# Query and key rows copied straight from SBUF rows into the SBUF stacks, in transfers of 64 KB, in a two-layer attention and expert kernel

## What is computed

```
x = x + attention0(layernorm(x), ctx, ctx)     # 16 heads of 16 channels, softmax(q.k/4 - 0.1*|t-t'|), then Wo
x = x + experts0(layernorm(x))                 # top 8 of 1024 small experts over 4 heads, plus a dense silu layer
x = x + attention1(layernorm(x), ctx, ctx)     # 16 heads, relu on q, k and v, softmax(q.k/4), no output projection
x = x + experts1(layernorm(x))                 # 8 experts of width 512, the 2 best per token
```

## Time and profile before

| | us |
|---|---|
| median of 3 runs | 1217.73 (1215.11 to 1217.9) |
| the profiled execution | 1213.62, of which the span is 1211.8 |
| PE busy in the span | 1055.4 (87%) |
| DVE busy | 788.4 (65%) |
| ACT busy | 638.7 (53%) |
| POOL busy | 474.4 (39%) |

### The profile page before, as it was taken

The page is one execution under the profiler, slowest core; times in us unless marked ns, Lnnn a source line. Parts: engine busy times, 40 slices in busy tenths (PEclk is TensorE's granted clock), DMA queues, the critical chain, the costliest instruction groups (busy, mean ns, idle before and its releaser), DMA issues.

```text
span 1211.8 us, 16920 instructions
## 1 busy us (share of the span) xinstructions
PE 1055.4 (87%) x5478; PEld 658.8 (54%) x5478; DVE 788.4 (65%) x1986; ACT 638.7 (53%) x848; POOL 474.4 (39%) x494
## 2 busy tenths in 40 slices
PE   9499899989776999999999778999999888799991
PEld 5134343434355787787777554433334334588881
DVE  3667677786489777877787334777777955244443
ACT  2146565566528667667677422565545661355550
POOL 1347777686413243343443321212323334222220
PEclk9579999999879999999999986999998998899996
DMA  7946778666999300000002330455453328222226
GB/s 186 249 148 192 228 198 264 174 206 224 255 238 233 78 1 1 1 1 1 1 1 64 103 78 1 148 165 146 117 167 93 102 63 325 66 74 71 72 62 209
DMA packets 75595, 151.71 MB, mean 125 GB/s; under 512 B 8234, under 2 KB 45356, under 8 KB 73974
## 3 DMA queue, kind: packets, MB, share of 16 engines
q1 hardware_dynamic: 62518, 99.46, 31.9%
q0 software_dynamic: 10544, 47.23, 11.2%
q10 hardware_dynamic: 2448, 3.94, 1.2%
HBM read 73.88 MB, written 76.25 MB: 124 GB/s over the span
## 4 chain that ended last, share of the span: by engine, by line
PE 55%; DVE 24%; ACT 8%; issue 6%; POOL 3%; DMA 3%; SPq 1%; ACTq 0%; DVEq 0%; POOLq 0%
PE ps L1296 14%; DVE negmax L1589 9%; PE ps L1194 7%; PE ps L1161 6%; PE ps L1140 4%; PE ps L1175 4%; PE ps L1149 4%; PE ps L1398 3%; PE ps L1375 3%; PE ps L1361 2%; PE ps L1203 1%; PE ps L1516 1%; DVE moe_w L1885 1%; DVE hl L1594 1%; DVE on L1609 1%
## 5 line engine op out<-in xcount | busy, mean ns | idle before, releaser
L1589 DVE TENSOR_REDUCE negmax<-ps 128x1 f32<-128x512 f32 x512 | 320.9, 682 | 68.9 <-PE ps L1161 67.2
L905 ACT ACTIVATE pt<-ps 128x1024 f32<-128x1024 f32 x256 | 256.4, 1026 | 129.9 <-PE ps L1175 129.1
L1161 PE MATMUL ps<-sk,sq 56*128 56x512 f32 x512 | 166.5, 460 | 48.0 <-DVE negmax L1589 24.7
L1194 PE MATMUL ps<-pt,v_aug 128*32 128x512 f32 x1024 | 142.6, 620 | 1.2 <-POOL pt L670 0.8
L1161 PEld LDWEIGHTS ps<-sk,sq 56*128 56x128 f32 x512 | 75.7, 200 | 105.3 <-DVE negmax L1589 76.3
L1175 PE MATMUL ps<-sq,sk 57*128 57x512 f32 x512 | 127.1, 489 | 2.5 <-DVE negmax L1589 1.4
L670 POOL TENSOR_TENSOR pt<-pt,near 128x256 f32<-128x256 f32 x128 | 92.3, 728 | 76.0 <-ACT pt L905 75.7
L1175 PEld LDWEIGHTS ps<-sq,sk 57*128 57x128 f32 x512 | 50.1, 190 | 101.2 <-issue 72.4
L835 POOL DMA_INDIRECT expert_out<-yo,dest x39 | 38.2, 980 | 116.2 <-ACT yo L1080 104.5
L751 POOL TENSOR_TENSOR w_first<-w_first,moe_w 128x1024 f32<-128x1024 f32 x16 | 38.1, 2379 | 105.7 <-DVE pt L1877 105.0
L1361 PE MATMUL ps<-sel,hl 128*128 128x512 f32 x256 | 71.7, 412 | 5.6 <-DVE pt L1877 5.6
(11 more groups left out here) (284 smaller groups left out, 2008.2 us busy)
## 6 DMA issues: line engine op xcount, KB each, us to landing
expert_rows<-zero SPq DMA_DIRECT2D x3, 5586.0 KB, 58.0
expert_weights_split<-wst POOLq DMA_DIRECT2D x8, 2048.0 KB, 9.4
qk_rows<-hl SPq DMA_DIRECT2D x30, 512.0 KB
sq<-qk_rows SPq DMA_DIRECT2D x60, 192.0 KB, 4.6
sk<-qk_rows SPq DMA_DIRECT2D x60, 192.0 KB, 5.1
moe_w<-in_w POOLq DMA_DIRECT2D x16, 512.0 KB, 7.1
wexp<-expert_weights_split POOLq DMA_DIRECT2D x16, 512.0 KB, 4.6
wexp<-expert_weights_split SPq DMA_DIRECT2D x4, 2048.0 KB, 17.1
```

What stands on the lines that cost most here:

```text
L905: act.activation(pt[:, 4 * (U % 2) + 2 * half:4 * (U % 2) + 2 * half + 2, :], ps[:, 2 + 2 * half:4 + 2 * half, :], ACT.Exp, scale=(BIAS, S ...
L1161: pe.matmul(ps[:, jbank(job), :], sq[r, pair, t * P:(t + 1) * P], sk[r, pair, :], start=True, stop=True).then_inc(s_job, 1)
L1194: ins = pe.matmul(ps[32 * j:32 * j + 32, OBANK, :], v_aug[:, b % 2, c, HG * g + j, :], pt[:, 4 * (U % 2) + j, :], start=(c == 0), stop=(c ...
L1589: dve.tensor_reduce(negmax[:, n % 2, col:col + 1], src, AX, ALU.max, negate=True).then_inc(s_jd, 1)
```

## The change

The DRAM tensor is gone, and so are `write_rows` and the wait for it. `stack` now copies 32 partitions of one part of `hl` (two head pairs by 16 channels) into 16 partitions by two pairs of a stack: 64 KB each, three for each of the four tiles, so 12 for a group of heads and 48 for a batch. For this the columns of the projection weights are permuted on the host so that a group's channels lie side by side. Each transfer adds 16 to `s_ld[g]`, so the counts waited for go from 64 to 192 for each batch, and ACT waits for the last group's `s_ld` before it overwrites `hl`; POOL waits for the last group of the last batch at step 41 of layer 1, where it had waited for the rows' write. The tables are new too: one `PREPARE` for all batches, `STACKS` at steps -10, -8, -4 and 0, `FINISH` one step later. At the start SP issues the 24 transfers of keys (behind three transfers of `x` and one of the context) and ACT the 24 of queries.

```
-PREPARE = {-22: ("xt", 0), -21: ("xt", 1), -20: ("k", 0), -17: ("k", 1), -16: ("q", 0), -15: ("q", 1), -13: ("v", 0), -12: ("v", 1)}
-PREPARE_SECOND = {-17: ("xt", 0), -16: ("xt", 1), -15: ("k", 0), -14: ("k", 1), -13: ("q", 0), -12: ("q", 1), -11: ("v", 0), -10: ("v", 1)}
-FINISH = {21: ("on", 0), 22: ("on", 1), 23: ("wo", 0), 24: ("wo", 1)}
+PREPARE = {-17: ("xt", 0), -16: ("xt", 1), -14: ("k", 0), -13: ("k", 1), -12: ("q", 0), -11: ("q", 1), -10: ("v", 0), -9: ("v", 1)}
+STACKS = {-10: 0, -8: 1, -4: 2, 0: 3}
+FINISH = {22: ("on", 0), 23: ("on", 1), 24: ("wo", 0), 25: ("wo", 1)}
...
-STACKS = (None, 10, 12, 12)
...
-            def write_rows(L, b, kind, s):
...
+            def stack(g, s, dst):
+                for i, part in enumerate((0, 1, 0) if dst is sq else (0, 0, 1)):
+                    at_row = HALF * s + DH * i
+                    sp.dma_start(dst[at_row:at_row + DH, 2 * g:2 * g + 2, :].bitcast(F32),
+                                 hl[2 * DH * g:2 * DH * (g + 1), s if dst is sq else 2 + s, part].bitcast(F32)).then_inc(s_ld[g], 16)
...
             def first_rows():
...
                 for s in range(2):
                     const_rows(1, s, sq)
-                sp.wait_ge(s_dw, 128 * (B + 1))
-                for g in range(NG):
-                    for s in range(2):
-                        stack(1, 0, g, s, sq)
+                for s in range(2):
+                    sp.wait_ge(s_pre, 3 + s)
+                    for g in range(NG):
+                        stack(g, s, sq)
...
-                        pool.wait_ge(s_dw, 128 * 2 * B)
+                        pool.wait_ge(s_ld[NG - 1], 192 * 2 * B)
...
-                        act.wait_ge(s_dw, 128 * (B * L + job.b))
+                        act.wait_ge(s_ld[NG - 1], 192 * (B * L + job.b))
...
             def first_stacks(g):
-                if g == 0:
-                    act.wait_ge(s_dw, 128)
-                for i, dst in ((1, sq), (3, sk)):
-                    src = rows[0, 0, i].rearrange("l (i e) t -> (l i) e t", e=NPAIR)
-                    act.dma_start(dst[HALF:HALF + BROW, 2 * g:2 * g + 2, :].bitcast(F32), src[:, 2 * g:2 * g + 2, :]).then_inc(s_ld[g], 16)
+                for s in range(2):
+                    if g == 0:
+                        act.wait_ge(s_jd, at[0, "q", 0, s].done)
+                    for i, part in enumerate((0, 1, 0)):
+                        at_row = HALF * s + DH * i
+                        act.dma_start(sq[at_row:at_row + DH, 2 * g:2 * g + 2, :].bitcast(F32), hl[2 * DH * g:2 * DH * (g + 1), s, part].bitcast(F32)).then_inc(s_ld[g], 16)
```

More of the change, by code:

```diff
@@ L131 @@
 BUSY = {LASTU + 5: 7, LASTU + 13: 2}
[L132 to L138 removed]
+STEPS = (range(-LEAD, LASTU + 10), range(-LEAD, LASTU + 18))
+NEXT_CTX = (-LEAD, -8)
 def attention_jobs():
@@ L412, in build @@
         s_job = sem("job_psum"); s_jd = sem("job_emptied_dve"); s_ja = sem("job_emptied_act")
-        s_hi = sem("qk_high"); s_dw = sem("rows_written"); s_ld = [sem(f"stack_in{g}") for g in range(NG)]
+        s_hi = sem("qk_high"); s_ld = [sem(f"stack_in{g}") for g in range(NG)]
         s_mr = [sem(f"max_rows_in{i}") for i in range(2)]
@@ L458, in load_ctx @@
                 sp.dma_start(ctxT[:, b % 2], kcut(a["ctx"][b])).then_inc(s_ctx[b % 2], 16)
-            def write_rows(L, b, kind, s):
[L461 to L469, removed]
+            def stack(g, s, dst):
[3 more added lines that the diff above has]
+                                 hl[2 * DH * g:2 * DH * (g + 1), s if dst is sq else 2 + s, part].bitcast(F32)).then_inc(s_ld[g], 16)
             def load_stacks(L, b, g):
-                if b:
-                    sp.wait_ge(s_st, 2 * (LASTU * L + NU * (b - 1) + 4 * g + 3) + 2)
-                if g == 0:
-                    sp.wait_ge(s_dw, 128 * (B * L + b + 1))
+                sp.wait_ge(s_st, 2 * (LASTU * L + NU * (b - 1) + 4 * g + 3) + 2)
                 for s in range(2):
[L477 to L482, removed]
+                    if g == 0:
+                        sp.wait_ge(s_jd, at[L, "k", b, s].done)
+                    stack(g, s, sk)
+                for s in range(2):
+                    if g == 0:
+                        sp.wait_ge(s_jd, at[L, "q", b, s].done)
+                    stack(g, s, sq)
             def load_max(L, b, g):
@@ L506, in first_rows @@
                     const_rows(1, s, sk)
-                for g in range(NG):
-                    for s in range(2):
-                        stack(1, 0, g, s, sk)
                 for s in range(2):
-                    write_rows(1, 0, "q", s)
+                    sp.wait_ge(s_pre, 1 + s)
+                    for g in range(NG):
+                        stack(g, s, sk)
                 sp.wait_ge(s_f, NTL)
@@ L534, in attention @@
                             load_max(L, b, (u + 2) // 4)
[L535 to L539, removed]
+                        if b and u in STACKS:
+                            load_stacks(L, b, STACKS[u])
                         if b + 2 < B and u == NEXT_CTX[b]:
@@ L2019, in layout @@
     expert = np.arange(NE).reshape(NX, 2, YK).transpose(1, 0, 2).reshape(-1)
-    order = np.array([(2 * e + s) * DH + ch for s in range(2) for ch in range(DH) for e in range(NPAIR)])
+    order = np.array([(2 * e + s) * DH + ch for s in range(2) for g in range(NG) for ch in range(DH) for e in (2 * g, 2 * g + 1)])
     return {
```

22 lines of the change are left out of this document (6 added, 16 removed).

## The result

The changed kernel takes 1240.36 us (median of 4 runs, 1232.67 to 1243.75), the kernel before 1216.8 beside it (4 runs, 1215.11 to 1217.9): a ratio of 1.0186, 95% interval 1.0134 to 1.0238. Forecast were 1225 and a range up to 1232. The profiled execution took 1232.67, 19 us more than that of before; it is the fastest of its four, 7.7 us under their median, so the profile shows less of the loss than the median does.

What follows compares the result with a forecast made beforehand. The prediction took PE to bound the steady state. Its terms, -1 - 2.1 + 4 + 2.5 + 2.2 + 1.5 = +7.1 us, on a median of 1217.7 gave 1225 us, range 1211 to 1232.

Steps and rivals of the forecast that it cites:

- rival D: Much slower: engines lack room for bursts beside POOL's traffic, six of eight groups 3 us late; 1235 or above; chance 0.1.
- a reordering of its jobs can't bring much: Steady state of the attentions: PE is the bound, and the same matmuls stand in it after reordering.
- the 2.5 us of the normalisation: Step 16, attention 0: POOL's norm waits for the moved xt job and PE stands, once; +2.5 us (+1.5 to +3).
- between 0.47 and 0.60 I take 0.60: Cost of one new 64 KB stack transfer: 0.60 us (109 GB/s), 7.2 us of all 16 engines for a group.
- 1.3 us for each of the three: +4 (0 to +9): Layer 0, steps 8, 27/28 and 44: bursts meet POOL's stores ahead of the maxima, so scores by key wait; +4 us.
- The start, -1: Before PE's first score product: no writes of `hl` to wait for, new transfers instead; -1 us, range -7 to +5.
- The wait of rows 2, -2.1: PE's wait for stack rows at step 13 of layer 0 goes through earlier issue; -2.1 us (0 to -2.5).
- Group 3 out of `hl`, 0 to +4: Steps 15 to 18: group 3's burst must leave `hl` before ACT writes the next `k`; 0, to +4 under a store.
- Into attention 1, +2.2: Entry to attention 1: query transfers come later, so the first score and reduce are late; +2.2 us (0 to +4).
- POOL at step 41, +1.5 (0 to +3): Layer 1: POOL waits for batch 3's last group, its later work ends late and DVE waits; +1.5 us.
- B: Faster: new transfers overlap and cost only their issue (0.47 us), bursts are late nowhere; -5.6 us, 1212; chance 0.2.
- C: No change: transfers cost 0.60 us, but the start wins 5 and maxima are not late; -0.9 us, 1217; chance 0.24.

Runs made afterwards that it cites:

- e3: The kernel before, with its way through DRAM, given the changed tables (PREPARE, STACKS, FINISH, NEXT_CTX): 1224.8 us, ratio 1.0073.
- h4: The kernel before, with its way through DRAM, given the changed tables but with the xt jobs one step earlier: 1215.9 us, ratio 1.0011.
- i3: e3 with each scores-by-key product issued twice in steps 9 to 15 of attention 0: 1217.1 us, ratio 1.0004.
- i1: The changed kernel with every stack transfer cut in two, 24 of 32 KB a group: 1435.3 us, ratio 1.1791.
- e1: The changed kernel with group 1's burst issued at step -6, behind the maxima, instead of -8: 1256.1 us, ratio 1.0333.
- g1: The changed kernel with POOL's 2 MB stores in attention 0 moved to steps outside the stack bursts: 1224.1 us, ratio 1.0052.
- i4: The changed kernel with the maxima's transfers issued by ACT instead of SP, all stacks staying on SP: 1231.0 us, ratio 1.0124.
- g2: The changed kernel with ACT issuing the query transfers of batches 1 to 3, SP only the keys: 1218.6 us, ratio 1.0007.
- e2: The changed kernel with the two xt jobs of a batch one step earlier (-18, -17): 1243.3 us, ratio 1.0241.
- e4: The changed kernel with POOL's last expert weight loads in attention 1 at steps 49 to 63 instead of from 41: 1236.0 us, ratio 1.0148.

## Why the prediction was wrong, point by point

The direction was right (0.54 for slower) and rival D named the size, with a tenth of the chance. Of +7.1 forecast, +23.6 was measured. Three steps failed: the moved jobs, which were put at one wait, what bounds a new transfer, and the size of the wait for the maxima.

*First, "a reordering of its jobs can't bring much".* I read the earlier trace rows as PE's bound, and took the moved jobs at nothing but the 2.5 us of the normalisation. That wait came as forecast, 2.4 us between steps 16 and 17 (POOL held PE for 2.07). But the tables cost 8.4 us (e3), and moving `xt` back by one step returned 8.9 (h4). Behind that wait in e3, and once ahead of it, TensorE's clock was low: 0.80 in place of 0.97 over 50 us. That the clock has a part in it is shown by i3, where more products took less time; how large a part isn't. What made the clock fall at 118 us in e3, behind a wait of 0.90 us, when h4's stayed up behind one of 0.77, is open.

*Second, "between 0.47 and 0.60 I take 0.60, since the constants are the same kind of copy".* The rate came out as forecast, 110 GB/s, and for the wrong reason: 0.63 us is what a queue needs to issue one transfer, at half the engines' share (0.46, where I had put a full one), and i1 shows it to be a price by the transfer. Both my bounds, 0.47 for the issue and 0.60 for the engines, were below it. The engines' bound was wrong in itself: 110 GB/s at 0.46 of 16 engines is 15 GB/s for each, or 0.14 us for a row of 2 KB, where I had 0.30 from the constants. Two queues together made 184 GB/s. With this the burst of two groups is 15 us of one queue however idle the engines are, and the one move that was tried didn't hide it (e1).

*Third, the maxima: "1.3 us for each of the three: +4 (0 to +9)".* The mechanism was right: bursts ahead of maxima, meeting POOL's store at step 8. The size was not: PE waits 9.3 us at step 12, 1.6 at step 32 and 0.2 at step 44. By my figures the maxima of step 9 leave 7.2 us after the start of step 8 and are in 8 us later. Step 8 starts at 101.03; they left 12.5 us after that and were in 9.4 us later. Group 1's burst began on time, at 101.17. Of the 5.3 us by which the issue was longer, 3.9 are its last six transfers beside POOL's store (7.46 for 3.6), 0.7 the context load that now stands between burst and maxima, and the rest pauses and the rate. Without the store in the way 16 us come back (g1), with the maxima in another queue 9.3 (i4), with half of the burst in another queue 21.8 (g2). These overlap, since each also takes away work at half clock, and their sum is more than the loss.

*The start, -1:* -2.9, within its bounds. The first score product came at 41.37, 6 us earlier than before, but the next had to wait for DVE until 46.06. *The wait of rows 2, -2.1:* right, it is gone. *Group 3 out of `hl`, 0 to +4:* 0 in after, but only because PE was already late: as soon as something else was won it cost 8.2 us (e2).

*Into attention 1, +2.2:* right. The statistics ahead of the first maximum end 19.5 us later than before (728.45 against 708.92), the first maximum starts 22.4 later (731.49 against 709.08 in the earlier trace rows), so the entry cost 2.9. What no term of mine has: attention 1 then wins about 7 us back, from +22.8 at its first step to +15.7 at step 45. The new transfers don't explain it, since e3 wins 6.3 there without them. The two rows of after:

```profile
730.69 1.19 PE L1132 MATMUL ps<-sk,sq 56*128 56x512 f32 x3 [4.71 <-DMA sq<-hl]
731.49 4.87 DVE L1560 TENSOR_REDUCE negmax<-ps 128x1 f32<-128x512 f32 x8 [2.79 <-PE ps L1132]
```

*POOL at step 41, +1.5 (0 to +3):* the right place, mis-sized. POOL stands 36.88 us and DVE's statistics wait for it, as forecast; PE loses 3.85 us, and in e4 the loss is gone. The last group is issued in 8.1 us, not 7.2, and is in 10.3 us after its first issue (965.23), not 8.7:

```profile
965.23 4.03 SPq L458 DMA_DIRECT2D sk<-hl  x6
969.30 4.08 SPq L458 DMA_DIRECT2D sq<-hl  x6
```

```profile
975.57 0.63 POOL L746 DMA_DIRECT2D wexp<-expert_weights_split  x1 [36.88 <-PE ps L1132]
...
983.30 0.76 DVE L1525 BATCH_NORM_STATS2 st<-x_tok 128x6 f32<-128x256 f32 x2 [3.35 <-POOL x_tok L785]
984.70 0.67 PE L1132 MATMUL ps<-sk,sq 56*128 56x512 f32 x1 [3.85 <-DVE negmax L1560]
```

*The rivals.* B fails at its own condition (a transfer below 0.5 us), since one queue can't issue that fast. C fails with the late maxima. D came nearest, yet its reason, engines without room, is only half of it: they stood at 0.46 in the middle of the burst and were full once POOL's store came, and while the maxima were in flight. By the Trainium skill ("SBUF — State Buffer", Door 1) 16 partitions give 109 GB/s, and I had taken its agreement with the earlier trace rows for support. At the start the transfers that SP and ACT had in flight together landed on different partitions and made 184 GB/s, so that figure doesn't bound a burst of them.

## What to carry to other kernels

Before many small transfers take the place of a few large ones, multiply their number by the issue time of a like transfer in the trace, see what waits behind them in the same queue, and share them over two queues: the bytes were fewer here, and the queue's time decided. Where PE is busy all the time, still read the granted clock and the count of products beside it, also behind a short wait: after the same wait of 2.1 us for POOL the next 10 us ran at a mean clock of 0.52 in e3 and of 0.83 in g2. A wait that is repaired can lay the next one bare (e1, e2), so repairs are to be tried together too: of the combinations tried only that of all four beat the kernel before. Moving the stores and ACT's help (g1 and g2) without the other two wasn't tried.

## What the runs showed of the hardware

- A copy from SBUF to SBUF costs its queue 0.63 us at 64 KB and 0.71 at 32 KB, while SP issued loads of 192 KB from DRAM 0.47 apart. One queue moved 110 GB/s with them at an engine share of 0.46, two queues 184 at 1.09.
- More work on TensorE made the kernel faster: 28 products repeated in steps 9 to 15, 1224.8 to 1217.1 us in the medians.
- POOL's 2 MB store holds up another queue's small transfers: six took 7.46 us for 3.76 with rows of 16 KB in the store, and 6.71 with rows of 4 KB.
- A wait of PE of 0.90 us was followed by 10 us at the lower clock in e3 (118 to 128 us), one of 0.77 us at the same place by none in h4.
